# Two-layer graph network kernel on Trainium2: the second layer's scatter turned round, gathered rows as weights

## What is computed

```
h = relu(layernorm(x))
x = x + relu(relu((1 + eps) * h + sum over edges (h[src] into dst)) @ W1 + b1) @ W2 + b2)
h = relu(layernorm(x))
x = x + h @ w_self.T + sum over edges (h[dst] @ weights[type] into src)
```

## Time and profile before

| | |
|---|---|
| median of 3 runs | 1557.21 us (1554.61 to 1560.56) |
| the profiled execution | 1555.58 us |
| its span | 1553.6 us, 20995 instructions |
| TensorE matmuls busy | 976.2 us (63%), 4924 records |
| TensorE weight loads busy | 672.7 us (43%), overlapping |
| VectorE busy | 696.7 us (45%) |
| GpSimd busy | 848.3 us (55%) |
| ScalarE busy | 395.2 us (25%) |
| TensorE's granted clock, mean | 0.769 of 2.4 GHz |

### The profile page before, as it was taken

The page is one execution under the profiler, slowest core; times in us unless marked ns, Lnnn a source line. Parts: engine busy times, 40 slices in busy tenths (PEclk is TensorE's granted clock), DMA queues, the critical chain, the costliest instruction groups (busy, mean ns, idle before and its releaser), DMA issues. The chain is left out here.

```text
span 1553.6 us, 20995 instructions
## 1 busy us (share of the span) xinstructions
PE 976.2 (63%) x4924; PEld 672.7 (43%) x4925; DVE 696.7 (45%) x2173; ACT 395.2 (25%) x936; POOL 848.3 (55%) x829
## 2 busy tenths in 40 slices
PE   3635833767942395878698995166565655656576
PEld 2512421333521163555474444155454544545455
DVE  5824883545786384677595431022122222222224
ACT  6313712334510273556383430000000000000000
POOL 0275457576357676668600006566666666666662
PEclk9656975898975597998798997576776767666767
DMA  3432212222212222222302892111111111111113
GB/s 79 133 78 59 47 32 78 56 70 61 41 28 64 61 60 67 66 62 65 61 1 68 260 291 84 43 46 44 46 44 46 44 44 48 43 45 44 47 44 58
DMA packets 47251, 103.20 MB, mean 66 GB/s; under 512 B 15485, under 2 KB 26382, under 8 KB 46800
## 3 DMA queue, kind: packets, MB, share of 16 engines
q0 software_dynamic: 33024, 67.69, 17.8%
q1 hardware_dynamic: 13846, 33.16, 6.9%
q10 hardware_dynamic: 308, 1.60, 0.4%
HBM read 71.73 MB, written 30.65 MB: 66 GB/s over the span
## 5 line engine op out<-in xcount | busy, mean ns | idle before, releaser
L370 POOL DMA_INDIRECT gathered<-h_table,row_of x418 | 461.2, 1103 | 311.7 <-issue 114.0
L370 POOL DMA_INDIRECT gathered<-z_table,row_of x405 | 386.2, 954 | 367.4 <-DMA z_table<-spare 164.8
L821 PE MATMUL ps<-gathered,node_hot 128*125 128x128 f32 x1620 | 349.5, 361 | 252.6 <-issue 234.7
L821 PEld LDWEIGHTS ps<-gathered,node_hot 128*125 128x125 f32 x1620 | 297.1, 261 | 305.1 <-issue 303.6
L435 ACT ACTIVATE place_val_b<-place_hot,code_b 125x128 f16<-125x128 f16 x728 | 314.4, 518 | 440.8 <-DVE place_hot L619 308.1
L653 DVE TENSOR_SCALAR node_hot<-iota_f,key_of 128x250 f32<-128x250 f32 x405 | 135.5, 373 | 470.2 <-remote 283.1
L826 PE MATMUL ps<-node_hot,gathered 128*128 128x506 bf16 (+1 forms) x1254 | 249.0, 344 | 96.9 <-issue 95.5
L802 PE MATMUL ps<-chunk_hot,place_val_a 125*128 125x405 f16 (+2 forms) x728 | 211.5, 319 | 102.3 <-issue 93.0
L804 PE MATMUL ps<-chunk_hot,place_val_b 125*128 125x405 f16 (+2 forms) x728 | 209.5, 316 | 41.7 <-issue 38.4
L826 PEld LDWEIGHTS ps<-node_hot,gathered 128*128 128x128 bf16 x1254 | 125.4, 102 | 204.2 <-issue 139.9
L623 DVE TENSOR_SCALAR chunk_hot<-iota_h,chunk_f 125x405 f16<-125x405 f16 (+2 forms) x728 | 168.5, 309 | 28.4 <-issue 28.4
(11 more groups left out here) (133 smaller groups left out, 335.2 us busy)
## 6 DMA issues: line engine op xcount, KB each, us to landing
z_table<-spare SPq DMA_DIRECT2D x50, 448.0 KB
gathered<-h_table,row_of POOLq DMA_INDIRECT x418
gathered<-z_table,row_of POOLq DMA_INDIRECT x405
z_table<-spare SPq DMA_DIRECT2D x50, 52.0 KB
out<-x_sb SPq DMA_DIRECT2D x6, 224.0 KB
h_table<-gathered SPq DMA_DIRECT2D x1, 1092.0 KB
w_table<-spare SPq DMA_DIRECT2D x2, 512.0 KB
w_rel<-w_table SPq DMA_DIRECT2D x1, 1024.0 KB, 4.9
```

Of the source, the lines that this page charges most:

```text
L370: pool.indirect_dma_start(place if s == LAST else place.rearrange("p j d -> p (j d)"), None, z_table if s == LAST else h_table, bass.Indir ...
L821: last = T.matmul(psf[0:NP, bass.ds(offs[i] + half * D, D)], node_hot_of[s][:, k % HOTS[s], half * NP:(half + 1) * NP], gathered_of[s][:, ...
```

## The change

In the second layer a chunk's gathered rows become the weights and the selection matrix of 250 nodes is streamed past them in one matmul, as in the first layer. The sums then stand transposed in PSUM, features on partitions, 250 columns for each pair of tiles. So the product with w_self is also made transposed, 13 matmuls of up to 250 columns. At the end ScalarE copies each bank into h2T, TensorE turns its tiles back with transposes into the bank before it (the first into bank 7), and VectorE adds that bank to x_sb. Gathers, ring sizes and the making of selection matrices stay as they are.

```diff
+        self_added = sem("self_added")
+        sumT_ready = sem("sumT_ready")
+        sum_turned = sem("sum_turned")
...
@@ ScalarE, behind all else @@
+            act.wait_ge(self_added, 13)
+            act.wait_ge(nhot_used, RING[0] + sum(CHUNKS))
+            for g, (a0, a1) in enumerate(groups):
+                n = min(2, a1 - a0) * NP
+                nc.scalar.copy(h2T[:, a0 * NP:a1 * NP].rearrange("p (b n) -> p b n", n=n),
+                               ps[:, g, 0:(a1 - a0) * D].rearrange("p (b c) -> p b c", c=min(2, a1 - a0) * D)[:, :, 0:n]
+                               ).then_inc(sumT_ready, 1)
...
@@ VectorE, at the end @@
-            dve.wait_ge(nhot_used, RING[0] + sum(CHUNKS))
             for g, (a0, a1) in enumerate(groups):
+                dve.wait_ge(sum_turned, g + 1)
                 V.tensor_tensor(x_sb[:, a0:a1, :], x_sb[:, a0:a1, :],
-                                psf[0:NP, a0 * D:a1 * D].rearrange("p (t d) -> p t d", d=D), ALU.add).then_inc(out_ready, 1)
+                                ps[0:NP, (g - 1) % 8, 0:(a1 - a0) * D].rearrange("p (t d) -> p t d", d=D),
+                                ALU.add).then_inc(out_ready, 1)
...
@@ TensorE, add_up @@
-                    for half in range(2 if s == LAST else 0):
-                        last = T.matmul(psf[0:NP, bass.ds(offs[i] + half * D, D)],
-                                        node_hot_of[s][:, k % HOTS[s], half * NP:(half + 1) * NP], gathered_of[s][:, k, :],
-                                        start=False, stop=False, skip_group_check=True)
+                    if s == LAST:
+                        last = T.matmul(psf[:, bass.ds(offs[i], WIDE[s])], gathered_of[s][:, k, :],
+                                        node_hot_of[s][:, k % HOTS[s], :], start=False, stop=False, skip_group_check=True)
...
@@ TensorE, around the chunks @@
-            for t in range(TILES):
-                T.matmul(psf[0:NP, t * D:(t + 1) * D], h2T[:, t * NP:(t + 1) * NP], wsT[:, :], start=False, stop=False,
-                         skip_group_check=True)
+            for t in range(0, TILES, 2):
+                n = min(2, TILES - t) * NP
+                T.matmul(psf[:, t * D:t * D + n], wsT[:, :], h2T[:, t * NP:t * NP + n], start=False, stop=False,
+                         skip_group_check=True).then_inc(self_added, 1)
             rounds_rest(nc.tensor, LAST, add_up)
+            for g, (a0, a1) in enumerate(groups):
+                pe.wait_ge(sumT_ready, g + 1)
+                for t in range(a0, a1):
+                    last = T.transpose(ps[0:NP, (g - 1) % 8, (t - a0) * D:(t - a0 + 1) * D], h2T[:, t * NP:(t + 1) * NP],
+                                       ident[:, :])
+                last.then_inc(sum_turned, 1)
```

## The result

The changed kernel took 1544.71 us (median of 7 runs, 1538.90 to 1552.64) beside 1557.32 us for the kernel before (7 runs, 1554.61 to 1564.58): a ratio of 0.9924, 95% interval 0.9897 to 0.9951. Run a second time, later, it took 1541.63 beside 1558.32 us, 0.9906 (0.9872 to 0.9941). It is 0.8 to 0.9% faster. The forecast was 1548.2, with most weight on "within half a per cent". The profiled execution took 1544.71 us with a span of 1542.7, against 1555.58 and 1553.6.

The account below looks back on a forecast made before the run. No engine is full: GpSimd's gathers pause for TensorE's late counts, 35 pauses, 81 us. Terms -10 + 0.5 - 1 + 1.5 = -9.0 us, from the shown median 1557.2 to 1548.2; range for 8 in 10: 1538 to 1563.

Parts of the forecast that it names:

- within half a per cent: Outcome class: a change of under 7.8 us, not told from no change; chance 0.50, against faster 0.40 and slower 0.10.
- The length of a pause: GpSimd's wait for a free ring group lasts 0.80 + 0.151 n us after n gathers, working off what the gathers left.
- Fewer records, more counts, longer stretches: Second-layer chunks: halved records make counts about twice as frequent, stretches 15 to 20 gathers in place of ten; -10 us.
- 8 chunks run ahead, as before, and about 10 trickling: TensorE's advance over a stretch of 20 gathers: 8 chunks run ahead plus about 10 counts arriving while gathers are issued.
- The end of the chunks: TensorE behind the last gather: +0.5 us for a longer last stretch, about 1 us less for the 30 chunks left.
- The start of the stage: The 13 wide self products hide behind the first five gathers and cost nothing more.
- The turn back: Copy, transposes and hand-overs before the first add at the end: +1.5 us, bounds 1.2 and 5; the rest hidden.
- Stretches of ten: Rival: GpSimd still pauses after every ten gathers, only the ends change; 1557 to 1558 us, chance 0.23.
- No more pauses: Rival: counts come at least every 1.25 us, the ring is never full; 1465 us; no or far fewer pauses, chance 0.12.
- slower rival: Two: GpSimd's stretches shrink to five, 1572 to 1600 us; last TensorE burst at lower clock, 1559 or 1568; together 0.10.

Follow-up runs that it names:

- 128, 224 and 288 columns in the changed kernel: Changed kernel with a memset of 128 partitions by that many columns behind each second-layer gather: 1550.09, 1543.5 and 1564.85 us (the last in one execution).
- the rows were halved: Changed kernel with second-layer gathers of 64 rows in place of 128, number of gathers kept: 1561.52 us in one execution.
- the kernel before with 224 columns: Kernel before with a memset of 128 by 224 on GpSimd behind each second-layer gather: 1555.91 us, ratio 1.0002.
- the cut product: Changed kernel with each chunk's wide product made as two of 125 columns, eight records a chunk again: 1556.6 us, ratio 1.0009.
- the half product: Kernel before with the second half of each chunk's product left out, four records a chunk in the old orientation: 1540.28 us in one execution.
- with 15 matrices: Changed kernel with 15 selection matrices in place of 9: 1542.75 us, ratio 0.9902; on another, faster chip 1322.32 us, ratio 1.0008.
- the memset of 1 column: Changed kernel with a memset of 128 partitions by 1 on GpSimd behind each second-layer gather: 1544.9 us.
- the kernel before with 15 matrices: Kernel before with 15 selection matrices in place of 9, on the faster chip: 1325.83 us in one execution.

## Why the prediction was right, step by step

**The length of a pause: right.** 0.80 + 0.151 n gives 3.82 for 20 gathers and 9.86 for 60; measured 3.6 to 4.0 and 9.87. The reading behind it, that a pause works off what the gathers left, held when the period was changed on its own (128, 224 and 288 columns in the changed kernel) and when the rows were halved. It doesn't cover the kernel before with 224 columns, which paused about 1 us seven times at a period above 1.40. Two readings of mine were off by little: from the first gather's start to the last there are 404 periods, 506 us, so the pauses make up 82 us and not 81, and with the one of 1.67 us there are 36 of them.

**Fewer records, more counts, longer stretches: right, and shown** by the cut product and the half product. Deep in a stretch the interval halved exactly, 11.2 to 5.6. The stretch came out at 20, the upper end of 15 to 20, and that is in part luck, out of two terms that were both off. I had put 8 chunks run ahead, as before, and about 10 trickling; from 1227.41 on TensorE ran 15 chunks in one burst and 5 trickled. The prediction gave the halved records to the trickle alone; they doubled the burst as well, from 8 chunks to 15 at some 30 matmul records. The late interval didn't fall from 4.2 to 2.1: 2.1 to 3.5 is the middle of the longer stretch, 4.9 its end. The gain of this step was 10.7 us against 10 forecast.

**The end of the chunks: mis-sized.** "+0.5 - 1" was -4.2. The last stretch is not longer on average: gather 400 is a multiple of ten and of 20, so the last pause is followed by five gathers before and after. And I took the waiting behind the last gather as fixed. Before, TensorE's burst stopped and took up again 2.1 us after the last gather's start, with 30 chunks at 0.505. Now it runs from 1514.26 without a break, and 61 of its records, again 30 chunks, start behind the last gather and are done in 13.06 us, 0.43 a chunk: 2.1 of waiting and 15.16 - 13.06 = 2.1 of work less. So the chunks themselves came out near the lower bound of 0.43 that I had given, not at the "about 1 us less" taken. Narrow matmuls don't run at that rate: the cut product's last 132 records took 17.97 us, 0.54 a chunk. In three other traces of the new form (the changed kernel again, with 15 matrices, and with the memset of 1 column) TensorE ended 14.6, 11.9 and 14.9 us behind the last gather, so against the one trace of the kernel before this term is -2.4 to -5.4.

**The start of the stage: right.** The wide self products start at 939.16 and end before the first chunk; nothing waits for them.

**The turn back: right.** 1.46 us from TensorE's end (1532.05) to the first add (1533.51) against 1.5. Seven copies in 3.14 us and 25 transposes in 3.21 lie beside 6.22 us of output DMA issues, 0.44 each.

**The sum.** -9.0 forecast; -13.5 in the stage, of which the late start of the execution compared took 2.6 back. On the medians it is -12.6. The forecast of 1548.2 missed by 3.5 us, most of it the end term, and that also moved the case from "within half a per cent", the likeliest class by a little, to "faster".

**The rivals.** Stretches of ten is what the cut product gives, 1.8 us above the kernel before measured beside it; 1557 to 1558, up to 1 above, was worked out. No more pauses happened in two ways: with slower gathers on this chip, where it brings nothing beyond the change, and on the chip at 1321 us, where the kernel before with 15 matrices has none to lose (with nine there is only its time there, 1321.30 us, and no trace). So at the gathers' own period it was not the records, as that rival (1465 us) had it, that decided whether GpSimd pauses at all; only with the memset of 224 columns did eight records a chunk still pause and four not. Neither slower rival showed: the clock was 1.00 in the last burst (13 us, 62 records), and no stretch had five gathers but the last.

The Trainium skill (TensorE: Matmul & The Clock Gate, the section on the per-tile semaphore tail) prices a count at about 26 ns. By that rule alone the changed kernel and its cut form, with 405 counts each, take the same time; the runs disagree, 0.9924 against 1.0009 of the kernel before.

## What to carry to other kernels

Where gathers run back to back beside an engine and its counts come late in a way that its work doesn't explain, count the instructions between two counts, not their columns: one wide matmul in place of two narrow ones doubled the rate of counts deep in a stretch, and the chunks run in a burst, at equal streaming. Before more is built on that, run the kernel on several chips, since the delay, and with it the gain, was absent on one (seen there with 15 matrices, which alone change nothing). And don't expect an average for the last stretch: work out on which instruction it begins.

## What was not expected of the hardware

- One kernel, two levels: the medians of the kernel before were 1554.8 to 1558.3 us in four of the five comparisons, and 1321.3 in one, on another chip. On the slower chips each gather instruction leaves 1.40 us of work whatever its rows (64 or 128), so that starts 1.252 apart pile up; on the faster one starts 1.259 apart pile up nothing. The same program, the changed kernel with 15 matrices, spans 1319.2 us on one and 1540.7 on the other; 152 of these 221 us lie ahead of the second layer's first gather (789.35 against 941.17) and 68 between its first and last. What makes the chips differ is open, and so is where the 1.40 us are spent. One rival for both is untested: every time here is of an execution whose spans and clock were recorded, and whether the recording itself makes instructions late on some chips no run tells.
- Deep in a pile, weight loads and matmuls pass at one record per 1.40 us: 11.2 / 8 in the kernel before and 5.6 / 4 after. It is the same 1.40 as a gather's, and it stays when gathers of 64 rows start 1.21 apart. That these are one thing (a record let through per gather worked off) is argued from these equalities alone.
- A memset of 0.12 us between two gathers costs nothing; one of 0.22 us makes the period 1.34, one of 0.30 makes it 1.42 (medians).
